# Four of the sixteen down-weight low halves move from GpSimd to VectorE in an attention and expert kernel

## What is computed

```python
x = x + xattn(layernorm(x), ctx_1024, ctx_1024, mask, ...)      # 16 heads of 64, 154 keys
x = x + ffn(layernorm(x), ...)
# ffn: a soft mixture of E = 16 experts with S = 64 slots each, D = 256, F = 512
logits = einsum("bnd,esd->bnes", x, se)
dispatch = softmax(logits, axis=1)
combine = softmax(logits.reshape(B, N, -1), axis=-1)
slots = einsum("bnd,bnes->besd", x, dispatch)
gate = gelu(einsum("besd,edf->besf", slots, Wg) + bg, approximate=False)
up = einsum("besd,edf->besf", slots, Wu) + bu
eout = einsum("besf,efo->beso", gate * up, Wd) + bd
out = einsum("bns,bso->bno", combine, eout)
```

## Time and profile before

| what | us |
|---|---|
| median of 3 runs | 552.45 |
| the runs | 552.14 to 552.88 |
| span of the profiled execution, first to last instruction | 550.3 |
| median less span | 2.15 |
| PE busy | 533.1 (97%) |
| DVE busy | 432.9 (79%) |
| ACT busy | 403.1 (73%) |
| POOL busy | 310.1 (56%) |

### The profile page before, as it was taken

The page is one execution under the profiler, slowest core; times in us unless marked ns, Lnnn a source line. Parts: engine busy times, 40 slices in busy tenths (PEclk is TensorE's granted clock), DMA queues, the critical chain, the costliest instruction groups (busy, mean ns, idle before and its releaser), DMA issues.

```text
span 550.3 us, 11967 instructions
## 1 busy us (share of the span) xinstructions
PE 533.1 (97%) x3896; PEld 499.6 (91%) x3896; DVE 432.9 (79%) x1301; ACT 403.1 (73%) x1098; POOL 310.1 (56%) x331
## 2 busy tenths in 40 slices
PE   7999999999999999999998999999999999989997
PEld 4889999999999999999997888999988877889997
DVE  6787878787897979899668998898698688755553
ACT  5879969596896959689564546689978888656562
POOL 6665654534544455454366768885569999910000
PEclk9999999999999999999999999999999999999999
DMA  8635000000020000000001343150288887515651
GB/s 257 185 77 174 3 1 2 2 2 1 9 90 2 2 2 0 4 0 4 0 1 79 152 186 140 61 198 25 82 273 273 268 301 246 179 55 186 181 164 68
DMA packets 34901, 54.11 MB, mean 98 GB/s; under 512 B 3997, under 2 KB 21497, under 8 KB 34713
## 3 DMA queue, kind: packets, MB, share of 16 engines
q1 hardware_dynamic: 34841, 53.36, 29.3%
HBM read 40.54 MB, written 10.49 MB: 93 GB/s over the span
## 4 chain that ended last, share of the span: by engine, by line
PE 69%; POOL 18%; ACT 4%; DVE 3%; issue 3%; SPq 2%; DMA 2%; POOLq 0%; DVEq 0%; ACTq 0%
PE ps L1577 8%; PE ps L1352 8%; PE ps L1364 8%; PE ps L1544 7%; PE ps L1456 7%; POOL w_gu_low L785 7%; PE ps L1491 6%; PE ps L1434 5%; POOL wkq_low L785 5%; PE ps L1468 4%; PE ps L1493 3%; PE ps L1636 2%; PE ps L1602 2%; POOL prob L721 2%; DMA wvo_raw<-in_L_xattn_Wo_dram 2%
## 5 line engine op out<-in xcount | busy, mean ns | idle before, releaser
L721 POOL TENSOR_TENSOR prob<-expo,prec 128x512 f32<-128x512 f32 x64 | 66.7, 1043 | 93.2 <-DVE prec L1143 92.0
L882 ACT ACTIVATE expo<-expo,nmin 128x154 f32<-128x154 f32 x256 | 106.2, 423 | 5.3 <-DVE nmin L1132 4.8
L1132 DVE CUSTOM_DVE_ANT_0 expo<-ps,maskb 128x154 f32<-128x154 f32 x256 | 69.0, 312 | 11.9 <-PE ps L1456 11.7
L1152 DVE TENSOR_TENSOR pT_low<-ps,pT_high 128x512 fp32r<-128x512 f32 (+1 forms) x96 | 57.3, 597 | 5.9 <-ACT pT_high L896 5.5
L1456 PE MATMUL ps<-kbd,qT_high 128*128 128x308 f32 x256 | 61.1, 323 | 0.0
L896 ACT CAST pT_high<-ps 128x512 fp32r<-128x512 f32 (+1 forms) x96 | 49.2, 514 | 13.5 <-PE ps L1468 9.1
L785 POOL TENSOR_TENSOR w_gu_low<-w_raw,w_gu_high 128x1024 fp32r<-128x1024 f32 x17 | 50.8, 2990 | 13.8 <-ACT w_gu_high L832 13.8
L800 ACT ACTIVATE oT_high<-ps,bqv_c 128x256 fp32r<-128x256 f32 x64 | 29.9, 467 | 34.7 <-PE ps L1493 34.7
L882 ACT ACTIVATION_READ_ACCUMULATOR expo<-expo,nmin 128x1 f32 x256 | 50.3, 197 | 0.0
L1040 DVE TENSOR_TENSOR w_gu_low<-w_raw,w_gu_high 128x1024 fp32r<-128x1024 f32 x14 | 35.3, 2518 | 8.9 <-ACT w_gu_high L832 8.8
L1456 PEld LDWEIGHTS ps<-kbd,qT_high 128*128 128x128 f32 x256 | 39.8, 190 | 0.2
(11 more groups left out here) (240 smaller groups left out, 1733.1 us busy)
## 6 DMA issues: line engine op xcount, KB each, us to landing
logits_dram<-lsb SPq DMA_DIRECT2D x16, 512.0 KB, 2.6
w_raw<-in_L_ffn_Wg_dram SPq DMA_DIRECT2D x16, 512.0 KB, 3.7
w_raw<-in_L_ffn_Wu_dram SPq DMA_DIRECT2D x16, 512.0 KB, 4.5
w_raw<-in_L_ffn_Wd_dram SPq DMA_DIRECT2D x16, 512.0 KB, 4.7
lraw<-logits_dram SPq DMA_DIRECT2D x13, 512.0 KB, 3.8
out_dram<-gate SPq DMA_DIRECT2D x16, 128.0 KB, 2.2
kbd<-keys SPq DMA_DIRECT2D x12, 154.0 KB, 2.8
wvo_raw<-in_L_xattn_Wv_dram SPq DMA_DIRECT2D x2, 512.0 KB, 6.9
```

The lines of the kernel that those rows point to most:

```text
L721: pool.tensor_tensor(prob[:, n % 2, :, heads, :], expo[:, n % 2, pp, :, :, 0:P], prec[:, n % 2, pp].unsqueeze(3).to_broadcast([P, 2, 2, P] ...
L882: ins = act.activation(row, row, ACT.Exp, scale=-1.0, bias=nmin[:, n % 2, pp, j, h:h + 1], accum_out=psums[:, n % 2, pp, j, h:h + 1])
L1132: ins = dve.tensor_tensor_reduce(out=expo[:, n % 2, pp, j, h, :], in0=ps[:, s % NS, h * SK:(h + 1) * SK], in1=maskb[:, (2 * (n // QUADS) + ...
L1152: dve.tensor_tensor(pT[1][0:rows, n % 2, 2 * t:2 * t + tiles], ps[0:rows, NS + k % NT, 0:tiles * 2 * P].rearrange("p (t n) -> p t n", t=ti ...
```

## The change

The low halves of the down weights of experts 3, 6, 9 and 12 are made by DVE, behind `eo_low` of the expert two before (EO 1, 4, 7 and 10). They get a semaphore of their own, `down_low_dve`, since two engines can't raise one count in order; `low_no` counts down pieces apart for the two. POOL leaves these four out.

```diff
@@ LATER_EXPERTS_DVE
+DOWN_DVE = (3, 6, 9, 12)
@@ pieces
-    low_no = {(e, w): sum(1 for e0, w0 in pieces[:i + 1] if w0 == w and e0 >= 2) for i, (e, w) in enumerate(pieces)}
+    low_no = {(e, w): sum(1 for e0, w0 in pieces[:i + 1] if w0 == w and e0 >= 2 and (w < 2 or (e0 in DOWN_DVE) == (e in DOWN_DVE)))
+              for i, (e, w) in enumerate(pieces)}
@@ low_made
-        return (gate_low, up_low, down_low)[w], low_no[e, w]
+        return (gate_low, up_low, down_low_dve if e in DOWN_DVE else down_low)[w], low_no[e, w]
@@ gpsimd
         for e, w in pieces[6:]:
-            if w != 1:
+            if w == 0 or (w == 2 and e not in DOWN_DVE):
                 weight_low(e, w)
@@ vector, step "EO"
                 ins.then_inc(acc_free, 1)
+                if e + 3 < E and e + 2 in DOWN_DVE:
+                    weight_low(e + 2, 2)
```

More of the change, by code:

```diff
@@ L492, in program @@
     b_pick_ready, b_zeros = sem("b_pick_ready"), sem("b_zeros")
-    w_high, gate_low, up_low, down_low, b_high, b_low, eo_high = (sem(s) for s in (
-        "w_high", "gate_low", "up_low", "down_low", "b_high", "b_low", "eo_high"))
+    w_high, gate_low, up_low, down_low, down_low_dve, b_high, b_low, eo_high = (sem(s) for s in (
+        "w_high", "gate_low", "up_low", "down_low", "down_low_dve", "b_high", "b_low", "eo_high"))
     first_low = [[sem(f"first_low{e}{w}") for w in range(3)] for e in range(2)]
```

## The result

The changed kernel takes **547.99 us** (median of 4 runs, 547.91 to 548.73), the kernel before beside it 552.58 (4 runs, 552.14 to 552.88): a ratio of 0.9921 with an interval of 0.991 to 0.9933. Forecast were 548.0 in 547.2 to 550.9. The profiled execution has a span of 546.2 where before had 550.3: 4.1 us less, where the forecast had 4.4. The medians differ by more because the profiled execution of before was one of its quicker ones: in every run whose time and span are both on record the time lies 1.7 to 1.9 us above the span, so that execution took some 552.1.

The account below looks back on a forecast made before the run. PE mostly bounds the kernel, losing time to POOL in the expert stage: -3.64 - 1.07 = -4.7, less 0.3 for DVE's waits, -4.4; span 550.3 to 545.9, plus 2.15 gives 548.0 us, range 547.2 to 550.9.

Parts of the forecast that it names:

- 3.64 and 1.07 us: PE's waits for POOL: 3.64 us in iterations GU(8) to GU(15), 1.07 us at EO(14) and EO(15); both come back.
- From the span to the median: Last step of the sum: the median of the runs lies 2.15 us above the span, giving 548.0 from 545.9.
- part 1: POOL's work up to gate piece (15, 0): four moved pieces save 4 x (2.36 - 1.01) = 5.4 us.
- part 3: Stage end: POOL's last piece ends at 478.9, EO(14) would start at 479.70, so 1.07 us comes back.
- part 2: Gate piece (15, 0) is ready at 471.8, wanted at 473.8: 2.0 us of slack, so all 3.64 come back.
- part 4: DVE's moved piece ahead of hT_low and hid takes 2.2 us with half an instruction's wait, inside 2.66 in hand.
- first rival: DVE's new piece mostly waits for a whole POOL instruction, hid 0.71 us late four times: 550.6 us; chance 0.16.
- part 5: ACT and weight transfers: ACT's 1.11 us wait shrinks; cost between 0 and 0.2 us an expert, taken as 0.
- The new piece mostly waits: DVE's piece blocked by a whole POOL instruction each time, 2.8 us lost of 4.7: 550.6 us; chance 0.16.
- The shared side is not relieved: The moved piece holds what DVE and POOL share as long on DVE as on POOL: 552.45 us; chance 0.08.
- DVE becomes the bound: DVE too slow from expert 3 to 14, once its pieces average above 2.7 us: 558 us; chance 0.06.
- Transfers: Weight transfers set the pace, 0.2 us for each of seven late iterations, 1.4 lost: 549.2 us; chance 0.05.

Follow-up runs that it names:

- up_zero: Kernel before, but DVE fills the low halves of the up weights of experts 2 to 15 with zeros, their products left out: 547.16 us.
- last_alone: Changed kernel with only the down piece of expert 14 on DVE, instead of those of 3, 6, 9 and 12: 551.25 us.
- one_middle: Changed kernel with only the down piece of expert 9 on DVE: 551.22 us.
- three_pieces: Changed kernel with the down pieces of experts 6, 9 and 12 on DVE, without that of expert 3: 548.32 us.
- all_on_dve: Changed kernel with all twelve down pieces of experts 3 to 14 on DVE instead of four: 551.52 us.
- every_second: Changed kernel with six down pieces on DVE, those of experts 3, 5, 7, 9, 11 and 13: 551.13 us.
- four_late: Changed kernel with the four down pieces on DVE being those of experts 9, 10, 11 and 12: 552.50 us.
- one_early: Changed kernel with only the down piece of expert 3 on DVE: 552.06 us.
- behind_hid: Changed kernel with DVE's four down pieces one place later, behind the next hid instead of ahead of hT_low and hid: 553.22 us.
- two_pieces: Changed kernel with two down pieces on DVE, those of experts 3 and 9, instead of four: 550.62 us.
- four_early: Changed kernel with the four down pieces on DVE being those of experts 3, 4, 5 and 6: 551.21 us.

## Why the prediction was right

**What PE loses to POOL: 3.64 and 1.07 us.** Both were there, with sizes a little off. up_zero, where POOL is never late, shows 3.43 in the stage and 1.20 behind it; the change gave 3.36 and 1.00, together 4.36, where the sum had 4.7 less 0.3 for DVE's waits. That the chain was 64 us of POOL and only some 3.5 us of it could be had is borne out. For the tail, last_alone shows the cause, against the releaser that the row names.

**From the span to the median: luck.** The sum ended at a span of 545.9 and added 2.15 us. The span was 546.2, and the time of that execution lies 1.8 above it; the 2.15 came from one execution of before that was quicker than its median. The two deviations cancel, so that 547.99 against 548.0 says less than it seems. The missing 0.3 is largely the 0.23 us by which the stage began later; that start varies between the profiled executions here, from 412.8 to 414.3 us in the kernels that do the whole work.

**What a piece is worth: right in its size, wrong for one of the four (part 1).** One_middle measured 1.36 for 1.35. But "4 x 1.35 = 5.4 us" treated all four alike, and expert 3's piece gives about 0.2: POOL has no queue of high halves there, and it idles for ACT in place of the piece. The total came out at 63.70 - 58.32 = 5.4 all the same, because of something I had not counted: the end of POOL's run moved ahead of one of DVE's up pieces, at 471.08, and so left out one hold of 1.01. Three pieces make 3 x 1.35 + 1.01 = 5.06 by this reading, and three_pieces measured 5.01. The total was right by two errors that cancel. One row was also misread: the up piece at 422.33 that took 1.23 did meet a POOL instruction. It started 0.10 ahead of POOL's gate piece at 422.43, which took 3.35 to the next start, so it was POOL that waited.

**The tail (part 3): right in the main, one step wrong.** That hold was only put off. The next down piece took it, 3.35 us in place of 2.36, and POOL's last piece was done at 477.77 + 2.39 = 480.16 and not at 478.9. EO(14) started 0.15 behind that, about as far as before (484.27 and 484.41), so it still waits some 0.2 us for POOL by this reading: 1.00 of the 1.20 came back.

**The slack (part 2) held.** Piece (15, 0) was ready at 472.07, forecast 471.8. It is used near 474.3, by the third pass of the GU(15) that starts at 473.34, some 0.95 in. Three pieces, with (15, 0) ready at 472.36, leave nearly the same slack; so they do as well as four within what can be told.

**DVE's queue (part 4).** Taken were 2.2 us for the moved piece, and it took 1.23, 2.65, 2.42 and 2.66, mean 2.24. The first found POOL idle; the other three took 2.58 on average, more than a wait of half an instruction. The 2.66 in hand shrank to 439.81 - 439.65 = 0.16 us in the second, 0.15 in the third and 0.15 in the fourth of these iterations. Where an HT stands 2.3 us for `hid` it also starts 0.14 to 0.15 behind it (all_on_dve, every_second, four_late), so these distances mean that the slack was used up to the last. It needs two iterations to come back: the next two HTs follow their `hid` by 1.15 and 2.65 us, which is why a piece in every third iteration does not add up. PE's twelve iterations from HT(2) to HT(14) sum to 62.87 us, 0.29 above 12 x 5.215. But the same twelve sum to 62.80 in up_zero, where none waits for `hid`: of the 0.3 that I gave back for DVE, most is PE's own pace, 5.23 and not 5.215, and only about 0.1 is DVE, in the iterations of 5.30 and 5.27 that end 0.15 behind `hid`. So the forecast was right, but with no margin left, and nearer to its first rival than the text has it.

**Transfers (part 5): nothing.** ACT's longest wait for a down weight is 0.33 us against 1.11 before.

**The rivals.** *The new piece mostly waits* did not happen in full in these four places: three of the four pieces waited, 1.2 to 1.4 us, and PE hardly felt it. But it is the mechanism of the kernels that failed: in four_late, every_second and all_on_dve one bad meeting, not four, cost 4 us, not 0.71 each. DVE had no lead left when its down piece was blocked in full: it had spent it on a down piece in the iteration before (four_late, all_on_dve) or on an up piece blocked in full (every_second); and behind the wait the granted clock fell to its lower level. *The shared side is not relieved* is ruled out by one_middle: had the piece held it as long on DVE, POOL's run would have stayed 63.70 long. The Trainium skill's caution (Perfetto Trace Analysis, Optimizing Scalar/DVE Operations), that moving work between these two engines "might not help", gives 0 here; measured are 4.6 us, and the measurement decides. It comes true in this case where POOL has no queue, as in one_early, and where the moved pieces make PE wait, as in four_late and behind_hid. *DVE becomes the bound* did not happen even with twelve pieces: their mean with the up pieces is (32.0 + 17.0) / 26 = 1.9 us, under the 2.7 from which I had it decide. PE waited for DVE there all the same, once for 2.29 us. *Transfers* are ruled out by the row above.

Of my expectations for the experiments, five of twelve missed clearly (two_pieces, four_late, behind_hid, all_on_dve, every_second) and four_early by 0.2 us. Three of these (four_late, all_on_dve, every_second) have one reason: I reasoned with mean waits, while one instruction blocked in full in front of `hid` decides. For four_late I had foreseen an HT wait of 1 to 2 us; it was 2.32, and I had not counted the slow clock behind it.

## What to carry to other kernels

When two engines take turns at what they share, price a move from one to the other by the difference of the two holds (2.36 against 1.01 us here), and count it only where the engine that gives has a queue standing; behind an idle place it is worth nothing. Then look at the receiving engine's queue: not whether it is full on average, but whether the slack ahead of its next awaited result takes one whole blocked instruction, and spread the moved pieces so that it recovers between them. The longest run in the chain of waits says where to act, but what can be won is only what the bound engine loses beside it.

## What was new about the hardware

- A DVE piece with both inputs in SBUF that starts 0.01 to 0.10 us behind POOL's takes 3.4 to 3.5 us in place of 1.23, the whole of POOL's instruction more. The Trainium skill says that issue order decides who blocks (SBUF — State Buffer, Who interferes with whom); these rows agree, and show that a hundredth of a us is enough. The other way round, a DVE piece at 443.80 in the changed kernel, 0.09 ahead of POOL's at 443.89, takes 1.23 and POOL's 3.36.
- In up_zero DVE's fills, which read nothing, did not lengthen POOL's gate pieces at all: 2413 ns on average, beside 2405 for down pieces.
- A standstill of PE of 2.3 us was followed by a granted clock of 0.50 and 0.64 for 3.6 us, and the iteration behind it took 1.5 us longer, in every_second. In the kernel before, with its waits of 0.2 us, the granted clock is 1.00 from 440 to 482 us.
